# A two-layer graph network kernel on one core: the loop over pairs of graphs written out in full

## The reference

```python
# layer A
q, k, v = x @ Wq.T + bq, x @ Wk.T + bk, x @ Wv.T + bv
pros = softmax(where(adj == 0, -16384.0, q_h @ k_h.T))        # per head
z = v
for _ in range(4):
    z = 0.9 * (pros @ z) + 0.1 * v
x1 = layernorm(x + z) * gamma + beta
# layer B
nx = ln1(x1); q, k, v = nx @ wq + bq, nx @ wk + bk, nx @ wv + bv
attn = softmax(q_h @ k_h.T / sqrt(32) + where(adj > 0, 0.1 * adj * adj, -inf))
x2 = x1 + (attn @ v) @ wo + bo
out = x2 + gelu(ln2(x2) @ w1 + b1) @ w2 + b2
```

## Time and profile before

| what | us |
|---|---|
| median of 3 runs | 2429.93 (2428.8 to 2429.98) |
| the profiled execution | 2428.21 |
| its span, first to last instruction | 2426.4 |
| TensorE busy | 2280.2 (94%) |
| ScalarE busy | 1924.3 (79%) |
| VectorE busy | 1718.6 (71%) |
| GpSimd busy | 1503.6 (62%) |

### The profile page before, as it was taken

One profiled execution on the slowest core, in us unless ns is written; L12 is line 12 of the kernel. 1 busy time (PEld: TensorE's weight loads), 2 busy tenths in 40 slices (PEclk: granted clock), 3 DMA queues, 4 the chain that ended last, 5 costly groups with the idle time before them and its releaser, 6 DMA issues.

```text
span 2426.4 us, 80248 instructions
## 1 busy us (share of the span) xinstructions
PE 2280.2 (94%) x29492; PEld 2164.7 (89%) x29492; DVE 1718.6 (71%) x7329; ACT 1924.3 (79%) x6462; POOL 1503.6 (62%) x1610
## 2 busy tenths in 40 slices
PE   2799999999999999999999999999999999999987
PEld 2689999999999999999999999999999999999986
DVE  2577777777767777767777767767767767776863
ACT  0678888888878888878888888878888888887964
POOL 0676666666666666666666666666666666666651
PEclk9999999999999999999999999999999999999999
DMA  3110010110011011011011011011011011011000
GB/s 93 34 33 30 27 37 24 32 37 30 26 37 29 26 37 36 19 36 37 19 37 36 19 36 37 19 37 36 19 37 36 19 37 36 24 32 36 19 15 14
DMA packets 95661, 76.63 MB, mean 32 GB/s; under 512 B 9601, under 2 KB 95105, under 8 KB 95361
## 3 DMA queue, kind: packets, MB, share of 16 engines
q1 hardware_dynamic: 95360, 71.87, 9.7%
HBM read 55.06 MB, written 16.78 MB: 30 GB/s over the span
## 4 chain that ended last, share of the span: by engine, by line
PE 84%; issue 4%; ACT 3%; DMA 3%; DVE 2%; POOL 1%; SPq 1%; POOLq 0%; ACTq 0%; DVEq 0%
PE ring_ps L337 36%; PE ring_ps L454 15%; PE ring_ps L400 12%; PE ring_ps L392 9%; PE score_ps L383 5%; PE ring_ps L420 5%; PE ring_ps L347 3%; DMA adj_A<-in_adj_dram 2%; ACT probs L490 1%; POOL x1b L774 1%; POOL rstd L759 1%; DVE n L667 0%; ACT hidden L518 0%; ACT hT_high L518 0%; DVE x L680 0%
## 5 line engine op out<-in xcount | busy, mean ns | idle before, releaser
L490 ACT ACTIVATE probs<-probs,negmax 128x128 f32<-128x128 f32 x2048 | 795.4, 395 | 11.7 <-DVE negmax L599 4.7
L750 POOL TENSOR_TENSOR probs<-probs,rinv 128x512 f32<-128x512 f32 x512 | 529.4, 1055 | 108.1 <-DVE rinv L613 108.1
L490 ACT ACTIVATION_READ_ACCUMULATOR probs<-probs,negmax 128x1 f32 x2048 | 395.8, 193 | 0.0
L504 ACT ACTIVATE zT<-ring_ps 128x512 f32<-128x512 f32 x256 | 158.3, 618 | 231.4 <-PE ring_ps L400 231.4
L337 PE MATMUL ring_ps<-inT_C_high,w_high 128*128 128x256 f32 x1024 | 301.3, 294 | 4.5 <-ACT hT_high L518 3.0
L392 PE MATMUL ring_ps<-ident,probs 128*128 128x128 f32 x2048 | 293.7, 276 | 7.2 <-POOL probs L750 4.5
L454 PE MATMUL ring_ps<-w_high,hT_high 128*128 128x256 f32 x1024 | 296.8, 290 | 0.9 <-DVE x L680 0.5
L673 DVE TENSOR_TENSOR hT_low<-hidden,hT_high 128x512 fp32r<-128x512 f32 x256 | 230.3, 900 | 87.3 <-ACT hT_high L518 83.4
L454 PE MATMUL ring_ps<-w_low,hT_high 128*128 128x256 f32 x1024 | 286.5, 280 | 0.0
L454 PE MATMUL ring_ps<-w_high,hT_low 128*128 128x256 f32 x1024 | 286.2, 279 | 0.0
L337 PE MATMUL ring_ps<-inT_C_high,w_low 128*128 128x256 f32 x1024 | 284.9, 278 | 0.0
(11 more groups left out here) (149 smaller groups left out, 7379.2 us busy)
## 6 DMA issues: line engine op xcount, KB each, us to landing
xT_sb<-in_xT_dram SPq DMA_DIRECT2D x64, 256.0 KB, 3.3
x_sb<-in_x_dram SPq DMA_DIRECT2D x64, 256.0 KB, 2.9
out_dram<-x SPq DMA_DIRECT2D x128, 128.0 KB, 1.7
adj_A<-in_adj_dram SPq DMA_DIRECT2D x64, 128.0 KB, 3.1
adj_B<-in_adj_dram SPq DMA_DIRECT2D x64, 128.0 KB, 2.1
probsT_A<-in_L_gnn_w_dram SPq DMA_DIRECT2D x1, 1024.0 KB, 7.7
probsT_B<-in_L_gnn_w_dram SPq DMA_DIRECT2D x1, 1024.0 KB, 10.1
probs<-in_L_gnn_Wq_dram SPq DMA_DIRECT2D x1, 256.0 KB, 2.8
```

The costliest lines, as they stand in the source:

```text
L490: e = act.activation(probs[:, u, h, :], probs[:, u, h, :], ACT.Exp, bias=negmax[:, u, h:h + 1], scale=-1.0, accum_out=sums[:, u, h:h + 1])
L504: act.activation(zT[k][:, :, :, :], ring(name).rearrange("p (b c n) -> p b c n", b=GB, c=C), ACT.Copy).then_inc(s_out[name], 1)
L750: pool.tensor_tensor(probs[:, u, hs, :], probs[:, u, hs, :], rinv[:, u, hs].unsqueeze(2).to_broadcast([P, HR, P]), ALU.mult).then_inc(s_pr ...
```

## The change

The loop and its helpers are gone. A `Timetable` lists all steps of all 69 bodies with the pair that each works on, in the same cyclic order, and each engine's program is written out from it. The count of every wait is a constant, every transfer has a constant address, and the buffers that alternate are chosen by the pair's number. `wait_apart` (with its tile) and `through` (with its semaphore) are removed. The bank of a step is its place in the list of all steps that really run, modulo 4. There are 32 such steps in a full body, so the banks of the full bodies go round as before; in the bodies at both ends, where steps are absent, they now rotate over the steps that are there.

```diff
-class Body:
-    def __init__(self, i, pairs=None, odd=None):
...
-    def before(self, order, name, apart):
...
+class Timetable:
+    def __init__(self, pairs):
+        self.steps = [(n, i - lag) for i in range(pairs + DEPTH) for n, lag in ENTRIES if 0 <= i - lag < pairs]
+        ringed = [s for s in self.steps if KINDS[s[0]][0] in RINGED]
+        scores = [s for s in self.steps if KINDS[s[0]][0] == "scores"]
+
+        self.bank = {s: i % RING for i, s in enumerate(ringed)}
+        self.before = dict(zip(ringed[RING:], ringed))
+        self.before.update(zip(scores[1:], scores))
...
-        def run(eng, steps):
-            head = DEPTH + 1 + (G - DEPTH - 1) % 2
-            for i in range(head):
-                steps(Body(i, G))
-            with eng.Fori(head, G - 1, 2) as i:
-                steps(Body(i, odd=head % 2))
-                steps(Body(i + 1, odd=(head + 1) % 2))
-            for i in range(G, G + DEPTH):
-                steps(Body(i, G))
...
-        def walk(body, does):
-            for name in body.names:
+        def run(does):
+            for name, g in table.steps:
                 kind = KINDS[name]
                 if kind[0] in does:
-                    does[kind[0]](name, *kind[1:])
+                    does[kind[0]](name, g, *kind[1:])
...
-                def load_adj(name, l):
-                    if body.later(name):
-                        sp.wait_ge(s_mask[l], body.count(name, 1))
-                    sp.dma_start(adj_sb[l][:, :, :], adj_v[body.pair(name)]).then_inc(s_adj[l], 16)
+            def load_adj(name, g, l):
+                if g:
+                    sp.wait_ge(s_mask[l], g)
+                sp.dma_start(adj_sb[l][:, :, :], adj_v[g]).then_inc(s_adj[l], 16)
...
-                def take(name):
-                    old, back = body.before(RING_ORDER, name, RING)
-                    if old:
-                        pe.wait_ge(s_out[old], body.count(old, back))
+            def take(name, g):
+                if (name, g) in table.before:
+                    old, h = table.before[name, g]
+                    pe.wait_ge(s_out[old], h + 1)
...
-                def wait_apart():
-                    n = next(spares)
-                    dve.memset(spare[:, n:n + 1], 0.0)
...
-                def through():
-                    pool.sem_inc(s_through, 1)
```

More of the change, by code:

```diff
@@ new lines, in turn, with input_ready @@
+            def turn(name, g, l):
+                src, ready = (nx, s_nx) if l == "B" else (n2, s_n2)
+                pe.wait_ge(ready, g + 1)
+                take(name, g)
+                for c in range(C):
+                    for b in range(GB):
+                        at = (c * GB + b) * P
+                        mm = pe.transpose(ring(name, g)[:, at:at + P], src[:, b, c * P:(c + 1) * P], ident[:, :])
+                mm.then_inc(s_full[name], 1)
+            def input_ready(g, l):
+                if l == "A":
+                    pe.wait_ge(s_split, g + 1)
+                else:
+                    emptied(g, "tB")
@@ L425, in attend, with hop @@
+            def hop(name, g, k):
+                if k:
+                    emptied(g, f"h{k - 1}")
+                else:
+                    emptied(g, "vA")
                     for half in range(2):
                         for b in range(GB):
[L427 to L436 removed]
@@ L458, in steps, with turn_back @@
-                walk(body, {"turn": turn, "project": project, "values": values, "scores": scores, "turn_probs": turn_probs,
-                            "hop": hop, "turn_back": turn_back, "attend": attend, "output": output, "up": up, "down": down})
-            run(pe, steps)
+                            emptied(g, f"pA{b}{half}")
+                mix(name, g, z[k - 1] if k else v_A[g % 2], probsT_A[g % 2])
+            def turn_back(name, g, k):
+                emptied(g, f"z{k}")
+                take(name, g)
+                for b in range(GB):
+                    for c in range(C):
+                        at = (b * C + c) * P
+                        mm = pe.transpose(ring(name, g)[:, at:at + P], zT[k][:, b, c, :], ident[:, :])
+                mm.then_inc(s_full[name], 1)
@@ new lines, in attend, with output @@
+            def attend(name, g):
+                emptied(g, "vB")
+                for half in range(2):
+                    for b in range(GB):
+                        emptied(g, f"pB{b}{half}")
+                mix(name, g, v_B, probsT_B)
+            def output(name, g):
+                emptied(g, "pv")
+                take(name, g)
+                for b in range(GB):
+                    mm = by_parts(ring(name, g)[:, b * H:(b + 1) * H], lambda a, kc: oT[a][:, b, kc, :],
+                                  lambda a, kc: wo_p[a][:, kc, :], C)
+                mm.then_inc(s_full[name], 1)
@@ new lines, in exps, with turn_probs @@
+            def exps(name, g, l, b, half):
+                u = UNIT[l, b]
+                act.wait_ge(s_masked[f"m{l}{b}{half}"], g + 1)
+                for h in range(half * HR, (half + 1) * HR):
+                    e = act.activation(probs[:, u, h, :], probs[:, u, h, :], ACT.Exp, bias=negmax[:, u, h:h + 1],
+                                       scale=-1.0, accum_out=sums[:, u, h:h + 1])
+                if half == 1:
+                    e.then_inc(s_exp[name], 1)
+            def turn_probs(name, g, l, b, half):
+                if half == 0:
+                    full(name, g)
+                    dst = probsT_A[g % 2] if l == "A" else probsT_B
+                    act.activation(dst[:, b, 0:HR, :], ring(name, g).rearrange("p (h n) -> p h n", h=HR),
+                                   ACT.Copy).then_inc(s_out[name], 1)
@@ L527, in _ @@
+            run({"turn": turn, "project": project, "exps": exps, "turn_probs": turn_probs, "hop": hop,
+                        "attend": attend, "up": up})
         @block.vector
@@ new lines, in values, with maxima @@
+            def values(name, g, l):
+                if l == "A" and g:
+                    dve.wait_ge(s_xv, g)
+                full(name, g)
+                row = bvA_row if l == "A" else bvB_row
+                dst = v_A[g % 2] if l == "A" else v_B
+                dve.tensor_tensor(dst[:, :, :], ring(name, g).rearrange("p (b n) -> p b n", b=GB),
+                                  row[:, :].unsqueeze(1).to_broadcast([P, GB, H]), ALU.add).then_inc(s_out[name], 1)
+            def maxima(name, g, l, b, half):
+                u = UNIT[l, b]
+                if b == 0 and half == 0:
+                    dve.wait_ge(s_full["s" + l], g + 1)
+                    dve.wait_ge(s_mask[l], g + 1)
+                for r in range(HR):
+                    h = half * HR + r
+                    t = dve.tensor_tensor_reduce(probs[:, u, h, :], score_ps[:, r, (b * C + half) * P:(b * C + half + 1) * P],
+                                                 mask[l][:, b, :], -1.0, HIGHEST, ALU.add, ALU.min,
+                                                 negmax[:, u, h:h + 1])
+                t.then_inc(s_masked[name], 1)
@@ new lines, in spread @@
+            def spread(name, g, n):
+                src = (y, x1, x2)[n]
+                if n == 1:
+                    dve.wait_ge(s_x1, g + 1)
+                else:
+                    dve.wait_ge(s_out["h3" if n == 0 else "o"], g + 1)
+                for b in range(GB):
+                    t = dve.bn_stats(stats[n][:, b, :], src[:, b, :])
+                t.then_inc(s_stats[n], 1)
+                dve.wait_ge(s_stats[n], g + 1)
+                for b in range(GB):
+                    t = dve.bn_aggr(moments[n][:, b, :], stats[n][:, b, :])
+                t.then_inc(s_moments[n], 1)
@@ new lines, in down @@
+            def down(name, g, b):
+                full(name, g)
+                if b == 0:
+                    dve.wait_ge(s_x2b, g + 1)
+                dve.tensor_tensor(x2[:, b, :], ring(name, g)[:, 0:H], x2[:, b, :], ALU.add).then_inc(s_out[name], 1)
+            run({"edge_bias": edge_bias, "turn": turn, "values": values, "maxima": maxima, "recip": recip,
+                        "turn_probs": turn_probs, "turn_back": turn_back, "attend": attend, "output": output,
+                        "spread": spread, "norm": norm, "low": low, "down": down})
```

634 lines of the change are left out of this document (248 added, 386 removed).

## The result

The kernel without the loop takes 2367.75 us in the median (2364.01 to 2368.66, 4 runs), the kernel before 2429.95 us beside it (2428.8 to 2433.88, 4 runs). The ratio is 0.9738, 95% interval 0.9721 to 0.9755: faster by 62 us. The forecast of 2349 us was 19 us too low and the time lies 6 us above the range.

A forecast was written before the change was run, and what follows sets the result against it. TensorE was taken to bound the kernel, interrupted by 28 loop branches; 2428.21 - 78.4 + 0.7 - 2 = 2348.5 us for the profiled execution, plus half a microsecond to the median: 2349 us, range 2345 to 2355.

The forecast's parts named there:

- What bounds the kernel, and the branches: At the loop's 28 branches back: TensorE sets 34.88 us per body; writing the loop out removes their cost, -78.4 us.
- What is late next: At the body boundary: tC's wait for n2 stays just in time through SyncE's shorter path; +0.7 us, ends 0 and 24.
- Fetching: Instruction packets: the straight program needs some 280 to 310, against 282 before, without slowing TensorE; 0 us.
- The helpers: Removed spare-column writes on VectorE and semaphore instructions on GpSimd: already hidden by TensorE, so 0, at most a microsecond.
- The banks: In the last bodies, TensorE's waits for ScalarE's reading shrink with banks four places back; -2 us, ends 0 and -7.0.
- R1: At body boundaries: slow loads open a 0.4 us wait for n2 20 to 59 times, +8 to +24 us; chance 0.14.
- R2: Before tC: the pause isn't the branch's and stays, only 2 us of branches go, 2424 to 2428 us; chance 0.03.
- R3: A rival in which the kernel gets slower; its place and size are not in the given text; chance 0.03.

The follow-up runs named there:

- e1: Written-out kernel with one unused 64-byte-per-partition tile allocated where the spare tile stood, no instruction changed: 2345.85 us, ratio 0.9641.
- e2: Loop kernel from before the change, helpers included, with the spare tile allocated behind all other tiles: 2465.43 us, ratio 1.0129.
- e3: Written-out kernel with the PSUM bank of each step chosen by its name, as before the change: 2370.21 us, ratio 0.9737.
- e4: Written-out kernel with the 320 spare-column writes and 192 semaphore instructions put back, spare tile allocated last: 2368.04 us in one run.
- e5: Written-out kernel with an unused 64-byte tile ahead of every named tile, so weights and activations move up together: 2364.29 us, ratio 0.9726.

## Why the prediction was right in kind and wrong in size

- *What bounds the kernel, and the branches (-78.4 us): right.* No "issue" pause of TensorE before `tC` is left, and with the addresses kept the 59 strides take 2057.92 us (e1), the number of the sum. From 2136.28 us that is -78.36.
- *What is late next (+0.7 us): right that nothing waits.* `n2` is 1.15 us early in the boundary shown, and `tC` waits only in the last four bodies. The sign of the small term can't be seen.
- *Fetching (0): right in effect.* 239 packets came on the one queue and 130 smaller ones on another (8 KB each), instead of 282 and 19; I had said 280 to 320. With them the stride of e1 is 34.88 us.
- *The helpers (0): right for their work, wrong for their memory.* Here the step failed. "The straight stretch shows that TensorE runs at 34.88 us" was carried over to the new program as if the 34.88 belonged to the list of products. I costed the 320 instructions that wrote `spare` and never the tile. Its removal moved all activations by 64 bytes against the weights: +0.34 us in 59 strides, +20.1 us. e1 (the tile alone put back) and e2 (the tile alone moved, in the loop kernel) show it from both sides.
- *The banks (-2 us): right in kind, too small.* e3 gives -4.4 us at the end. I had held ScalarE for the real limit behind these waits; in fact 3.8 of their 7.0 us went.
- *The start.* The first `d1` comes 2.0 us earlier (164.26 against 166.28), in no term of mine. e3 has 166.29 and e4, with the new banks, 165.78, so the banks aren't shown to be its cause. The granted clock differs while the first bodies fill (same stretch, before and after; the clock is the third number from the end):

```profile
103.00:108.00 5.00, 4.44 (x21) 4.04 (x20) 2.81 (x16) 3.78 (x17) 4.52 (x6) 0.50 0.54 148
103.00:108.00 5.00, 4.03 (x35) 3.74 (x32) 2.81 (x16) 4.67 (x20) 4.92 (x6) 1.00 0.53 149
```

  It is 0.50 in e3 and e4 too, and 1.00 in e1 (first `d1` at 164.38). e2 has 1.00 and still 165.51, so the clock fits most of these starts and not all; open.
- *The sum for the profiled execution:* 2428.21 - 78.36 + 20.06 - 2.02 - 3.87 = 2364.02, where -3.87 is the end (119.97 us after the last full `d1` against 123.84). Measured: 2364.01. So it was forecast 15.5 us too low: +20.1 for the tile, -2.0 for the start, -1.9 for the end beyond my -2, and -0.7 for the wait that did not come. The other 3.2 us of the miss in the median are the step from the profiled execution to the median, 3.7 us here where I had added half a microsecond.
- *The rivals.* R1 spoke of 2357 to 2373 us and of strides of 35.2 to 35.5, and both came; but its mechanism, a wait of `tC` for `n`, is absent. The number alone would have confirmed a wrong story, by luck; its second mark (`n` named as what is waited for) rejects it. R2 and the slower R3 are out: no pause before `tC` in the 59 strides, and a granted clock of 1.00 from 80 to 2280 us. None of my cases had the products themselves slower.

The slow clock stands in the forecast twice: as most of the 17.7 us (78.36 - 60.7) that the branches cost beside the idle array, and as about 1.9 us in the step to the median. Both are estimates: the 1.9 us are the difference of two strides (38.94 - 37.06 us), and no run shows the cost of the lower clock alone. What the traces show is the clock, 0.51 from 253.40 to 256.10 us after the pause that ended at 252.72 us, and the strides: of the 28 long ones in the kernel before eight are over 38 us.

The forecast gave the place of one operand against the other no worth. These runs disagree: 2.74 (e1) against 2.84 us (after) for the same 24 products, by the distance of their two operands. Where in the machine it arises, no run here shows.

## What to carry to other kernels

When a kernel is bound by TensorE back to back, compare the steps from product to product of the two profiles, not only its waits: an engine that is busy for all of a stretch can still have become slower (70.00 of 70.00 us here in both, with 924 products and then with 919). An edit that adds or removes a tile, used or not, moves the tiles allocated behind it (here `inT_C_high` from 105024 to 104960); keep their places (or put scratch tiles last from the start) when the edit is to be judged, and list what moved against what didn't. And where long runs of products have both operands in SBUF, try a few paddings of 64 bytes: here they took 45 us off the kernel after, some 20 of them lost by the change itself, where removing every branch was worth 78.

## What the runs showed of the hardware

- The pace of the 256-column products of fp32r (the type of the high and low parts) changed with the distance of their two operands' addresses: in full bodies from 113.3 to 120 ns each, for the same instructions in the same order at a granted clock of 1.00. Moving both by 64 bytes (e5) left the stride at 35.22 us and each group's pace within 0.1 ns of the kernel after. The turns of `probs` through `ident`, whose operands also came 64 bytes closer, kept their time (`pA11` takes 356 ns in e1 and in the kernel after).
- At the distance 192 modulo 256 a group took one of two paces, 113.3 or 117.8 ns, the same one in every full body of a written-out kernel, but not always in the loop kernel, where `u1` falls to 117.8 ns in bodies 54 and 62. Only groups at 192 and, in the bodies at the ends, at 64 were seen at 113.3 ns; what decides between the two paces is open.
- TensorE's branch back took 3417 ns in the median, and the array stood for 60.7 us at 28 of them; in the kernel written out in full `tC` waits at none of the 59 boundaries, and each stride is 35.22 us.
- In the loop kernel the lower clock (0.50 to 0.51) followed 8 of the 28 pauses, and 18 of them after a shift of 64 bytes (e2), with pauses of nearly the same length (63.6 us in all against 60.7).
